# Attention and feed-forward layer: first chunk of x loaded ahead, turns of x one output later, non-finite marks on ScalarE

## The reference

```python
xn = _layernorm(x)                                  # x is (2, 1024, 1024) float32
def bitnet_linear(x, weight, scale_param):
    s = jnp.maximum(jnp.mean(jnp.abs(weight), axis=1), 1e-08)
    y = jnp.einsum('bsi,oi->bso', x, jnp.sign(weight / s[:, None]))
    y = y * (s * scale_param)[None, None, :]
    return jnp.nan_to_num(y, nan=0.0, posinf=1000000.0, neginf=-1000000.0)
q, k, v = (bitnet_linear(xn, w, s) for w, s in (...))   # 1024, 256, 256 outputs
attn = softmax(q k^T / sqrt(32)) v                  # 32 heads, 8 key/value heads
out = x + bitnet_linear(attn, o_weight, o_scale) \
        + (silu(xn @ gate) * (xn @ up)) @ down      # 3584 wide, int4 weights in groups of 128
```

## Time and profile before

| | |
|---|---|
| time, median of 3 runs | 2496.96 us (2495.53 to 2497.45) |
| the profiled execution's own time | 2498.24 us |
| its span in the trace | 2496.4 us |
| PE busy | 2371.1 us, 95% of the span |
| DVE, ACT, POOL busy | 73%, 63%, 40% |
| mean granted clock of TensorE | 0.977 |

### The profile page before, as it was taken

How to read it: one execution, slowest core, us unless ns; L and a number is a source line. 1 busy time by engine, 2 the same in 40 slices (tenths; PEclk the granted TensorE clock), 3 DMA queues, 4 the chain that set the end, 5 groups by cost and what they waited for, 6 DMA issues and landing times.

```text
span 2496.4 us, 33125 instructions
## 1 busy us (share of the span) xinstructions
PE 2371.1 (95%) x12408; PEld 962.0 (39%) x12408; DVE 1810.4 (73%) x2326; ACT 1566.0 (63%) x2008; POOL 996.7 (40%) x553
## 2 busy tenths in 40 slices
PE   5698999999999999995999999999999999999998
PEld 3244333333333333322344444444444444444444
DVE  5577877777777777762547777777777777777777
ACT  5444377777777777784126666666665566666664
POOL 1111089999999999995002222221001222222000
PEclk9799899999999999997999999999999999999999
DMA  5201155555556555544121111113103111114111
GB/s 174 70 9 45 53 73 81 89 82 87 90 81 90 84 86 88 86 76 95 75 93 35 34 34 51 34 34 110 43 34 135 68 34 47 38 34 168 51 34 68
DMA packets 179851, 174.65 MB, mean 70 GB/s; under 512 B 87586, under 2 KB 127394, under 8 KB 179702
## 3 DMA queue, kind: packets, MB, share of 16 engines
q1 hardware_dynamic: 117430, 150.62, 19.1%
q0 software_dynamic: 62272, 22.03, 11.4%
HBM read 160.08 MB, written 65.45 MB: 90 GB/s over the span
## 4 chain that ended last, share of the span: by engine, by line
PE 90%; DVE 4%; issue 2%; ACT 1%; DMA 1%; POOL 1%; SPq 0%; DVEq 0%; ACTq 0%; POOLq 0%
PE ps L1394 31%; PE ps L1410 15%; PE ps L1238 10%; PE ps L1265 10%; PE ps L1254 9%; PE ps L1216 5%; PE ps L1277 4%; PE ps L1374 4%; POOL zone L525 1%; DVE zone L941 0%; PE ps L1426 0%; DMA zone<-in_L_attn_o_weight_dram 0%; PE ps L1202 0%; DVE zone L873 0%; PE ps L1194 0%
## 5 line engine op out<-in xcount | busy, mean ns | idle before, releaser
L1394 PE MATMUL ps<-xT,zone 128*128 128x512 f16 x3584 | 774.6, 379 | 3.6 <-DVE zone L1157 2.7
L965 DVE TENSOR_REDUCE zone<-ps 128x1 f32<-128x512 f32 x1024 | 638.7, 683 | 173.2 <-PE ps L1238 173.2
L721 ACT ACTIVATE zone<-ps,sm 128x512 f32<-128x512 f32 x1024 | 626.6, 691 | 182.0 <-PE ps L1254 180.1
L525 POOL TENSOR_TENSOR zone<-zone 128x1024 f32<-128x1024 f32 x256 | 633.4, 2584 | 176.7 <-ACT zone L721 103.6
L1134 DVE TENSOR_SCALAR ps<-ps,zone_c 128x1024 f32<-128x1024 f32 x392 | 506.8, 1293 | 161.4 <-PE ps L1394 159.3
L789 ACT ACTIVATE ps<-ps,zone_c 128x1024 f32<-128x1024 f32 x392 | 426.5, 1088 | 261.0 <-PE ps L1394 259.2
L1394 PEld LDWEIGHTS ps<-xT,zone 128*128 128x128 f16 x3584 | 350.2, 98 | 427.3 <-DVE zone L1157 4.2
L1238 PE MATMUL ps<-zone 96*128 96x512 f16 x1024 | 394.6, 388 | 5.1 <-DVE zone L965 4.6
L1254 PE MATMUL ps<-zone 98*128 98x512 f16 x1024 | 388.1, 382 | 4.1 <-ACT zone L721 4.0
L1410 PE MATMUL ps<-zone 128*128 128x512 f16 x1792 | 387.1, 379 | 0.0
L576 POOL CAST zone<-zone 128x1024 f16<-128x1024 f32 x56 | 58.0, 1037 | 724.5 <-DVE zone L1138 724.5
(11 more groups left out here) (127 smaller groups left out, 1358.3 us busy)
## 6 DMA issues: line engine op xcount, KB each, us to landing
zone<-dequantised SPq DMA_DIRECT2D x84, 512.0 KB, 3.6
dequantised<-zero_points SPq DMA_DIRECT2D x84, 256.0 KB, 4.1
zone<-zone SPq DMA_DIRECT2D x384, 32.0 KB, 2.3
zone<-_attn_hidden_states_dram SPq DMA_DIRECT2D x16, 512.0 KB, 8.2
zone<-inverse_sums SPq DMA_DIRECT2D x128, 64.0 KB, 2.2
attention<-zone SPq DMA_DIRECT2D x32, 256.0 KB, 2.0
xT<-attention SPq DMA_DIRECT2D x4, 2048.0 KB, 12.0
dequantised<-in_L_ffn_gate_w_dram POOLq DMA_DIRECT2D x28, 256.0 KB, 6.2
```

The lines of the kernel that those rows point to most:

```text
L525: nc.gpsimd.tensor_tensor(duo[n % 3], prob[:, e % 8, :], prob[:, (e + 2) % 8, :], add).then_inc(s["sum_ok"], 1)
L721: A(prob[:, e % 8, m % 2 * 512:(m % 2 + 1) * 512], ps[:, 3 + m % 3, :], ACT.Exp, scale=gam[:, 0:1]).then_inc(s["exp_ok"], 1)
L965: V.tensor_reduce(mxs[:, u % 2, half, i % 16:i % 16 + 1], ps[:, (2 * i + half) % 3, :], AX, amax).then_inc(s["max_ok"], 1)
L1394: last = MM(ps[:, 4 * s2 + 2 * m + c, :], ring[:, buf, m * H + g * P:m * H + (g + 1) * P], xT[:, hf, part, g, c * 512:(c + 1) * 512], star ...
```

## The change

On SP, the four tiles of x's first chunk are issued first, each with a semaphore of its own, then eight weight tiles, then chunk 1 of x; the zero points are stored ahead of chunk 3 of x, and ACT waits for that store only before `head` of the first k output. On DVE the moments are taken tile by tile as x lands; the clipping moves from POOL to DVE. The turns of chunk 0 use two pairs of banks (6, 7 and 2, 3). On PE only two weight tiles are turned ahead of x, the rest between the first four projections. The non-finite mark becomes an ACT instruction (`Abs` with scale 0, L664 of the changed kernel), behind each `evac_output`; outputs p >= 2 go through three buffers in place. The turns of the following chunk stand one output later: on PE in slots 6 to 10, on ACT in slots 6 to 11.

```diff
+            load_x(0)
+            for k in range(8):
+                load_w(k)
+            load_x(1)
...
             load_x(2)
-            load_x(3)
             sp.wait_ge(s["z_ok"], 1)
             sp.dma_start(zscr.rearrange("t m c -> t (m c)"), zf16).then_inc(s["z_out"], 16)
+            load_x(3)
...
-            def clip(c):
-                for i in range(4 * c, 4 * c + 4):
-                    pool.wait_ge(s["norm_ok"], i + 1)
-                    nc.gpsimd.tensor_scalar(x_tile(i), x_tile(i), 64.0, -64.0, amin, amax).then_inc(s["xp_ok"], 1)
...
+        def turn_bank(i):
+            return 2 if i in (1, 3) else 6
...
-            act.wait_ge(s["fac_ok"], 1)
-            act.wait_ge(s["z_out"], 16)
 
             def evac_output(c, p):
...
-                A(y2[:, p % 2, :], ps[:, output_bank(n), :], ACT.Copy, scale=cc[:, QKV[p]:QKV[p] + 1]).then_inc(s["y_ok"], 1)
+                A(output(p), ps[:, output_bank(n), :], ACT.Copy, scale=cc[:, QKV[p]:QKV[p] + 1]).then_inc(s["y_ok"], 1)
+                if n >= 1:
+                    act.wait_ge(s["r_ok"], n)
+                act.wait_ge(s["y_ok"], n + 1)
+                A(mask, output(p), ACT.Abs, scale=0.0).then_inc(s["mask_ok"], 1)
...
+            act.wait_ge(s["fac_ok"], 1)
             for c in range(NC):
                 i = 4 * (c + 1)
                 for p in range(12):
                     evac_output(c, p)
                     if p >= 3:
                         head(c, p - 1)
+                    if c == 0 and p < 2:
+                        for k in (8 + 2 * p, 9 + 2 * p):
+                            if k + 1 < NW:
+                                signs(k + 1)
+                            evac_weights(k)
...
                         elif p == 5:
                             high(i)
                             high(i + 1)
+                        elif p == 6:
                             evac_high(i)
-                        elif p == 6:
+                        elif p == 7:
                             evac_low(i)
+                            evac_high(i + 1)
                             high(i + 2)
-                            evac_high(i + 1)
-                        elif p == 7:
+                        elif p == 8:
                             evac_low(i + 1)
                             high(i + 3)
+                        elif p == 9:
                             evac_high(i + 2)
-                        elif p == 8:
+                        elif p == 10:
                             evac_low(i + 2)
                             evac_high(i + 3)
-                        elif p == 9:
+                        elif p == 11:
                             evac_low(i + 3)
...
+                for i in tiles:
+                    dve.wait_ge(s["norm_ok"], i + 1)
+                    V.tensor_scalar(x_tile(i), x_tile(i), 64.0, -64.0, amin, amax).then_inc(s["xc_ok"], 1)
...
-                guard(y2[:, p % 2, :], rv2[:, p, :] if p < 2 else r2[:, p % 2, :], fin).then_inc(s["r_ok"], 1)
+                ch.inc(V.tensor_scalar(clamped, output(p), 1e6, -1e6, amin, amax))
+                settle()
+                dve.wait_ge(s["mask_ok"], n + 1)
+                dve.nop(nofuse=True)
+                V.copy_predicated(output(p), mask.bitcast(i32), clamped).then_inc(s["r_ok"], 1)
...
-                        turn_weights(4 + 2 * p)
-                        turn_weights(5 + 2 * p)
+                        for k in ((2, 3), (4, 5), (6, 7, 8), (9, 10, 11))[p]:
+                            turn_weights(k)
                     if p == 3:
                         turn_values(c)
                     if c + 1 < NC:
-                        if p == 5:
+                        if p == 6:
                             pe.wait_ge(s["v_out"], 2 * c + 2)
                             turn_high(i)
-                        elif 6 <= p < 9:
-                            turn_low(i + p - 6)
-                            turn_high(i + p - 5)
-                        elif p == 9:
+                        elif 7 <= p < 10:
+                            turn_low(i + p - 7)
+                            turn_high(i + p - 6)
+                        elif p == 10:
                             turn_low(i + 3)
```

More of the change, by code:

```diff
@@ L282, in _ @@
                              allow_slow_non_contiguous=True).then_inc(s["par_in"], 16)
-            for k in range(4, 8):
+            for k in range(8, NW):
                 load_w(k)
-            load_x(1)
             for m, zsrc in enumerate((gz, uz)):
@@ L643, in _ @@
             evac_high(0)
+            high(2)
             evac_low(0)
-            high(2)
             evac_high(1)
+            high(3)
             evac_low(1)
-            high(3)
             evac_high(2)
@@ L652, in _ @@
             evac_low(3)
-            signs(4)
-            for k in range(4, NW):
-                if k + 1 < NW:
-                    signs(k + 1)
+            signs(2)
+            for k in range(2, 8):
+                signs(k + 1)
                 evac_weights(k)
-            act.wait_ge(s["fac_ok"], 1)
-            act.wait_ge(s["z_out"], 16)
             def evac_output(c, p):
@@ L671, in head @@
                 act.wait_ge(s["r_ok"], 12 * c + p + 1)
+                if (c, f) == (0, 8):
+                    act.wait_ge(s["z_out"], 16)
                 z, f0, k = (qz, b * 8 + f, 0) if f < 8 else (kz, b * 2 + (f - 8), 1)
-                A(z[:, f0, 0, s2 * 512:(s2 + 1) * 512], r2[:, p % 2, :], ACT.Copy, scale=fac[:, k:k + 1]).then_inc(s["h2_ok"], 1)
+                A(z[:, f0, 0, s2 * 512:(s2 + 1) * 512], output(p), ACT.Copy, scale=fac[:, k:k + 1]).then_inc(s["h2_ok"], 1)
             def evac_turned_values(c):
                 b, s2 = c // 2, c % 2
+                if c == 0:
+                    act.wait_ge(s["z_ok"], 1)
                 for fv in range(2):
@@ L881, in low @@
                                        mult, sub).then_inc(s["l_ok"], 1)
+            for i in range(4):
+                dve.wait_ge(s[f"x_first{i}"], 16)
+                moments((i,))
+            statistics(0)
             magnitude(0)
-            magnitude(1)
-            dve.wait_ge(s["x_in0"], 64)
-            moments(range(4))
-            statistics(0)
-            magnitude(2)
             inverse_deviation(0)
-            normalise(range(4))
-            magnitude(3)
+            normalise((0, 1))
+            normalise((2, 3))
             low(0)
             low(1)
-            magnitude(4)
+            magnitude(1)
             low(2)
-            magnitude(5)
+            magnitude(2)
             low(3)
+            for k in range(3, 6):
+                magnitude(k)
             for k in range(6, NW):
@@ L1279, in pair_sums @@
                 last.then_inc(s["dn_pe"], 1)
-            for k in range(4):
-                turn_weights(k)
+            turn_weights(0)
+            turn_weights(1)
             turn_high(0)
```

73 lines of the change are left out of this document (32 added, 41 removed).

## The result

The changed kernel takes **2482.92 us** (median of 5 runs, 2481.27 to 2489.72). The kernel before took 2496.38 (5 runs, 2495.21 to 2497.45) beside it. The ratio is 0.9953, 95% interval 0.9937 to 0.9968: 13.5 us faster. The profiled execution of the changed kernel is the longest of the five, 2489.72 us with a span of 2487.9; against the profiled execution of before it is 8.5 us faster. The five runs differ in their mean granted clock: 0.979 (2489.72), 0.981 (2486.43), 0.982 (2482.92), 0.983 (2481.27), 0.984 (2481.97).

The account below looks back on a forecast made before the run. PE is busy 95% of the span, so time can only be won where it waits or runs at the lower clock. 8.4 + 16.0 - 5.0 - 1.0 - 0 - 12.2 = 6.2 us faster: 2490.8, range 2478.0 to 2500.5.

Parts of the forecast that it names:

- Start: Up to chunk 0's first projection, P(0,0): it starts at 34.0 us, 8.4 earlier.
- P(0,0) to P(0,4): From chunk 0's first projection to its fifth: 27.3 us instead of 43.3, 16.0 saved.
- P(0,4) to P(1,0): From chunk 0's fifth projection to chunk 1's first: 45.5 us instead of 40.5, 5.0 lost.
- the three waits: Slots 9, 10 and behind 11: PE waits for evacuations behind evac_output on ACT, 2.85, 3.3 and 3.3 us.
- Chunks 1 and 2: Old waits of 5.30 and 6.48 go, new ones come: 55.5 us (1.0 lost) and 55.95 (0).
- Chunk 3 and behind: Chunk 3 has no turns and its outputs are paced by PE and the score rows: change of 0.
- a shift there as a sign of being wrong: The forecast is wrong if chunk 3 and the scores shift; no size given.
- Clock: PE's clock falls behind some of nine new waits, 1.35 us per wait: 12.2 lost, bounds 0 and 22.5.
- That the clock holds: Rival: the clock does not fall at the nine new waits; gain 18.4, time 2478.6 us; chance 0.15.
- That it stays low between waits: Rival: the clock does not recover between a chunk's last waits; 31 instead of 12.2 lost, 2509.6 us; chance 0.08.
- That PE waits for none of the nine: Rival: the turns' evacuations find a gap on ACT; 28.8 and 12.2 more gained, 2450 us; chance 0.06.
- That the start gives little: Rival: 5 to 8 us of the first two terms are missing; near 2497 us, no difference; chance 0.09.

Follow-up runs that it names:

- experiment seven: The changed kernel with one bank pair for chunk 0's turns again: 2494.39 us.
- Experiment three: The kernel before with only the zero points stored ahead of x's chunk 3 and waited for before the first k output's head: 2482.77 us.
- experiment five: The changed kernel with the non-finite mark computed twice on ACT for every output, the second waiting for the first: 2507.54 us.
- experiment one: The changed kernel with ACT's evacuations of x's turned parts one output earlier in slots 8 to 10, PE's order untouched: 2453.56 us.
- experiment two: The changed kernel with the non-finite mark back on DVE, none on ACT: 2470.87 us.
- (four): The changed kernel with the turns of x back in slots 5 to 9 on PE and ACT: 2471.72 us.
- (nine): The kernel of experiment one with the non-finite mark on DVE as well: 2451.69 us.
- experiment six: The changed kernel with x's clipping back on POOL: 2489.0 us.
- eight: The changed kernel with the first two weight tiles loaded ahead of x's first chunk, as before: 2484.37 us.

## Why the prediction held, and where it was off

**Direction, place and chain were right, the size was not.** I forecast 2490.8 (2478.0 to 2500.5), it is 2482.92: 13.5 us faster where I had 6.2. The profiled execution was put at 2492.0 and took 2489.72. That this one lies so close is in part luck: it is the longest of five, and errors of single terms, of up to 2.8 us and of both signs, partly cancel.

- *Start*: 8.4 forecast, 9.1 measured. The square root starts at 16.39 (forecast 16.5), the first `high` at 19.81 (19.85), P(0,0) at 33.33 (34.0). The clip takes 0.60 in a row on DVE (two in 1.29), not 0.72. The term holds two gains: experiment seven gives 3.5 to the bank pair, and 3.1 lie ahead of the first `high` (22.95 and 19.81). x was not there at 7.5, the estimate that I took from the Trainium skill's page "DMA: Bandwidth & Descriptors", section "Anatomy of one DMA — SWDGE (gpsimd) path": the third tile's moments, which waited for its data, start at 9.10 and the last tile's at 10.53. That section gives its figure for DMAs that GpSimd issues, and x is issued by SP, so the estimate took it further than the page does. Nothing in the sum hung on it.
- *P(0,0) to P(0,4)*: 15.4 of 16.0. (The terms written for the end of P(0,3) add up to 54.7, not 55.0.) The waits between, 1.61 for signs and 2.54 for the last evacuation, are the ones named. Experiment three isolates the store: 14.5 at the score row.
- *P(0,4) to P(1,0)*: the three waits, 2.85, 3.3 and 3.3 forecast, are 2.67, 3.11 and 3.07, ended by the evacuations named. The one in slot 6 is 2.65, not 4.6: PE came 0.9 later (72.5 instead of 71.65, part of a projection at the lower clock), and `high(4)` was done 1.1 earlier (75.0 instead of 76.1). Behind it stands a fall of the clock that the sum did not have: 1.7 in the projection of 5.30.
- *Chunks 1 and 2*: forecast 55.5 and 55.95 at full clock, measured 60.19 and 61.91. The waits of 5.30 and 6.48 went and the three waits came, as said; what is over, 4.7 and 6.0, is the clock: in chunk 1 1.7 in the projection of 5.30, 2.6 in that of 6.18, 0.4 in the turn of 1.01.
- *Chunk 3 and behind*: put at nothing, and wrong by 2.8: the lead is 5.7 at P(3,0) (forecast 6.2) and 8.5 at the end. The prediction had named a shift there as a sign of being wrong. No run isolates it.
- *Clock*: 12.2 forecast. In the profiled run it fell behind six of the nine waits and cost 12.4 (1.7 in chunk 0, 4.7 and 6.0 in the windows of chunks 1 and 2; half of the time that PE is busy at the lower level), 2.1 for each fall, near the six or seven of ten and 2.0 each of the forecast. **For the median this is the mis-sized term.** The profiled run is the longest of five; the median run is 6.8 shorter at a clock of 0.982 instead of 0.979. A clock that is 0.003 higher over 2488 us is 15 us less at the lower level, and half of that, 7.5, is time won if PE is busy in it: enough for the whole difference. So, as an estimate from clocks with three digits, the term was near 5 in the median run, and it was 12 in the longest of five. I had put the sum on one execution's clock as if it were the kernel's.

**The rivals.** That the clock holds (2478.6) came close: the shortest runs are within 3 us of it. That it stays low between waits (2509.6) never happened; behind each fall it was back after 3.5 to 7 us, and even waits of 3.6 to 3.8 in experiment five did not keep it low. That PE waits for none of the nine (2450) did not happen, since all nine are there; it is what experiment one makes of the kernel: 2453.56, so that rival's price was right to 4 us, and what it needed was another order on ACT. That the start gives little is refuted by P(0,0) and P(0,4).

**What the experiments add to the reasons.** The waits are ACT's order (one), the mark is 0.72 of each (two), the store of the zero points alone gives the whole gain (three), the later turns cost the changed kernel 11 us (four) although they remove the waits of 5.30 and 6.48, and the two costs of the change, the late slots and the mark, meet in the same nine waits: without the waits the mark costs 2 us or nothing (nine), with them 12 (two).

**Open.** Why the clock falls behind one wait of 3.1 us and not behind another was not settled, nor whether the clips on POOL bring it down more often, nor where the last 2.8 us come from. The kernel with x ahead and nothing else was not run.

## What to carry to other kernels

When work on a bound engine is moved later, follow it to the engine that must finish it: the turns had slack on PE, but their evacuations went behind an instruction that waits for PE itself, and PE then waited for the round trip, three times a chunk. An instruction added to an engine that is 63% busy cost 12 us inside such a round trip and 2 or nothing outside one; break the round trip first, then place the work. And a wait at the end of a stage hides lateness that was made earlier in it: when it is removed, look for the next one a few slots before.

## What the hardware showed

The clock can fall late. In the changed kernel PE stood from 90.39 to 93.06, and windows of PE alone (columns as in the earlier trace rows) read:

```profile
93.00:93.50 0.50, 0.44 (x8) 0.98 0.00 0
93.50:94.00 0.50, 0.50 (x6) 0.50 0.00 0
102.00:102.50 0.50, 0.50 (x9) 1.00 0.00 0
109.00:109.50 0.50, 0.46 (x3) 1.00 0.00 0
```

The fall to 1.2 GHz came 3.1 us after PE had stopped, when it was at work again, so the projection behind the wait pays for it (5.29 instead of 3.62). The next two waits, of 3.11 and 3.07, brought no fall. In chunk 1 the wait of 3.11, from 156.06 on, did, and earlier, while PE still stood:

```profile
158.00:158.50 0.50, 0.00 (x0) 0.83 0.00 0
```

The projection behind that one took 6.18. Over the profiled runs the clock fell in or behind 2 of 9 waits of 1.91 to 2.39 us (experiment two), 6 of 9 of 2.63 to 3.11 (the changed kernel) and 7 of 9 of 3.29 to 3.77 (experiment five), and in experiment one, whose waits at these places are 0.34 or none, behind none. The same nine waits of 2.63 to 3.11 in experiments six, seven and eight brought 7, 8 and 3 falls, so the count for one length of wait differs widely from run to run. The Trainium skill, "TensorE: Matmul & The Clock Gate", section "HAM oscillation — how this bites in real kernels", warns of long idle gaps, and all these waits up to 3.11 are shorter than the ones it means. Read as a promise that shorter ones cost nothing, it does not hold here: 26 of 45 waits of 1.91 to 3.11 us had a fall in or behind them.

DVE beside POOL: in experiment six a clamp of 128x512 at 62.28 took 1.26 us while POOL clipped, and two copies by the mark 1.36 and 1.35. In the changed kernel, where POOL does not clip, a clamp takes 0.41 to 0.43 and the copy 0.73. Not every instruction beside POOL is slow: the clamp at 66.38 took 0.41, though POOL clipped from 65.81 to 69.14. For PE the clips' place was worth under 1 us.
